# One FFN and attention kernel on one core: softmax in batches inside the attention turns, gathers ahead of the gate sums, row split one quarter later

## The reference

```python
def ffn(x):                       # x: (16384, 256)
    xn = x * rsqrt(mean(x * x) + eps) * norm_weight
    probs = softmax(xn @ router_w.T + router_b)          # 8 experts
    gates, idx = top_k(probs.T, cap)                     # cap = 2048 rows for each expert
    xe = xn[idx]
    hmid = gelu(einsum('ech,efh->ecf', xe, fc1_w) + fc1_b)      # 256 -> 1024
    ye = einsum('ecf,ehf->ech', hmid, fc2_w) + fc2_b            # 1024 -> 256
    out = zeros.at[idx].add(ye * gates)
    gate_sums = zeros.at[idx].add(gates)
    return out / maximum(gate_sums, 1e-9)

x = x + 0.5 * ffn(layernorm(x))
x = x + attention(layernorm(x))   # causal, per group of 512 rows, W_q, W_k, W_v, W_o
x = x + 0.5 * ffn(layernorm(x))
```

## Time and profile before

| | |
|---|---|
| median of 3 runs | 2108.49 us (2108.31 to 2108.55) |
| the profiled execution | 2110.22 us |
| its span, first to last instruction | 2108.4 us |
| mean granted TensorE clock | 0.954 |
| busy: TensorE, VectorE, ScalarE, GpSimd | 1920.1, 1472.9, 1423.7, 1239.9 us |

### The profile page before, as it was taken

The page is one execution under the profiler, slowest core; times in us unless marked ns, Lnnn a source line. Parts: engine busy times, 40 slices in busy tenths (PEclk is TensorE's granted clock), DMA queues, the critical chain, the costliest instruction groups (busy, mean ns, idle before and its releaser), DMA issues. The chain is left out here.

```text
span 2108.4 us, 41402 instructions
## 1 busy us (share of the span) xinstructions
PE 1920.1 (91%) x14844; PEld 1335.1 (63%) x14844; DVE 1472.9 (70%) x4305; ACT 1423.7 (68%) x2737; POOL 1239.9 (59%) x1353
## 2 busy tenths in 40 slices
PE   8628899999999999899999999238999999999997
PEld 6514556666666666577777777215666666666665
DVE  8788867677777765388888888787656555555542
ACT  8745556766767676578888887555676676666663
POOL 5213777677777776644444442024876767676665
PEclk9759999999999999999999999669999999999999
DMA  8932456464555454646555553215565655655443
GB/s 277 343 101 74 115 88 129 83 111 96 95 109 99 95 82 70 110 124 158 155 147 152 157 147 109 93 47 114 98 108 93 124 91 103 114 100 94 81 73 39
DMA packets 361742, 242.27 MB, mean 115 GB/s; under 512 B 228929, under 2 KB 348993, under 8 KB 361281
## 3 DMA queue, kind: packets, MB, share of 16 engines
q1 hardware_dynamic: 304192, 172.34, 31.0%
q0 software_dynamic: 57344, 67.29, 21.2%
HBM read 121.03 MB, written 84.93 MB: 98 GB/s over the span
## 5 line engine op out<-in xcount | busy, mean ns | idle before, releaser
L1251 DVE SCALAR_TENSOR_TENSOR hid_l<-hf,hid_h 128x512 f16<-128x512 f32 x512 | 351.2, 696 | 348.7 <-ACT hid_h L695 345.5
L1457 PE MATMUL ps<-w_h,hid_h 128*128 128x256 f16 x2048 | 558.8, 273 | 0.0
L1459 PE MATMUL ps<-w_h,hid_l 128*128 128x256 f16 x2048 | 558.7, 273 | 0.0
L1458 PE MATMUL ps<-w_l,hid_h 128*128 128x256 f16 x2048 | 558.7, 273 | 0.0
L799 ACT ACTIVATE hf<-ps,b 128x512 f32<-128x512 f32 x512 | 345.8, 675 | 83.5 <-PE ps L1459 76.4
L1457 PE MATMUL ps<-xt,w_h 128*128 128x512 f16 x1024 | 391.5, 382 | 8.3 <-ACT hf L799 8.3
L1458 PE MATMUL ps<-xt,w_h 128*128 128x512 f16 x1024 | 391.4, 382 | 0.0
L1459 PE MATMUL ps<-xt,w_l 128*128 128x512 f16 x1024 | 391.2, 382 | 0.0
L695 ACT ACTIVATE ys<-yb,weight 128x256 f32<-128x256 f32 x256 | 128.0, 506 | 344.3 <-DVE yb L1269 331.3
L695 ACT ACTIVATE hid_h<-hf 128x512 f16<-128x512 f32 x512 | 322.4, 630 | 16.2
L586 POOL DMA_INDIRECT weight<-gate_d,gate_at x256 | 257.6, 1006 | 82.1 <-issue 77.0
(11 more groups left out here) (295 smaller groups left out, 3879.9 us busy)
## 6 DMA issues: line engine op xcount, KB each, us to landing
w_st<-fc_t SPq DMA_DIRECT2D x32, 1024.0 KB, 5.6
xin<-x SPq DMA_DIRECT2D x32, 512.0 KB, 5.6
xa<-x_d SPq DMA_DIRECT2D x32, 512.0 KB, 4.5
out<-x SPq DMA_DIRECT2D x32, 512.0 KB, 5.2
z_d<-z SPq DMA_DIRECT2D x32, 512.0 KB, 6.0
xt<-xs SPq DMA_TRANSPOSE x256
weight<-gate_d,gate_at POOLq DMA_INDIRECT x256
b_st<-fc_b SPq DMA_DIRECT2D x16, 128.0 KB, 5.5
```

Of the source, the lines that this page charges most:

```text
L1251: dve.scalar_tensor_tensor(hid_l[:, n % 2, f, :], hf[:, f % HF, :], HS, hid_h[:, n % 2, f, :], ALU.mult, ALU.subtract).then_inc(s_hl, 1)
L1457: pe.matmul(dst, lh, rh, start=first, stop=False)
L1458: pe.matmul(dst, lh, rl, start=False, stop=False)
L1459: return pe.matmul(dst, ll, rh, start=False, stop=last)
```

## The change

Five things are changed.

1. Layer 1 gets four softmax batches (groups 0 to 16, 16 to 24, 24 to 28, 28 to 32). The first three run inside attention turns: shares_from in turns 22, 30 and 34, the exponential a turn later, shares two turns later. In route(1) seven of the eight transposes and the copy of 896 of 1024 columns run ahead of the fourth batch.
2. On GpSimd, both layers: the second half of the roots of chunk 0 stands between two halves of the gathers of chunk 1, the roots of chunk 1 right behind them, and the gathers of chunk 3 ahead of the gate sums; scatter(1) and scatter(2) go out in turns 3 and 4 ahead of the roots.
3. On VectorE: the statistics of chunk 1 ahead of count_slots(0, E0, 2), its shift ahead of the chunks; tile_of in two parts, one quarter ahead of the pick and three quarters behind the first quarter's work.
4. In layer 0, for m > 0: rows_hi, rows_shift and rows_lo of the next chunk in quarter 1 instead of quarter 0.
5. On TensorE: other_limits from quarter 3 of chunk 0 to quarter 0 of chunk 1.

```diff
@@ -83,7 +83,9 @@
     PER = P // NE
     RING = 4
     WIDE = 8
-    SOFT = (((0, 10), (10, 20), (20, 28), (28, 32)), ((0, 32),))
+    SOFT = (((0, 10), (10, 20), (20, 28), (28, 32)), ((0, 16), (16, 24), (24, 28), (28, 32)))
+    SOON = (22, 30, 34)
+    KEYED = NT // PER - 1
     assert KD == 2 and TG == 4 and NC == 4 and PER * NE == P and NT == P
 
     xf = x.rearrange("b s d -> (b s) d")
@@ -565,12 +567,12 @@
                 N0, E0 = layer * NC * NE, layer * NE
                 LAST = NC * NE
 
-                def gather(n):
+                def gather(n, t0=0, t1=TG):
                     E, c = divmod(n, NC)
                     pool.wait_ge(s_idx, n + 1)
                     wait(pool, s_xsl, TG * (n - 1))
                     pool.sem_inc(s_passed[0], 1)
-                    for t in range(TG):
+                    for t in range(t0, t1):
                         k = TG * c + t
                         landed = s_first[t] if n == N0 else s_xe[n % 2]
                         pool.indirect_dma_start(xe[:, n % 2, t, :], None, rows,
@@ -606,13 +608,14 @@
                     wait(pool, s_zst[u], 16 * (NG // 2) * layer)
                 gather(N0)
                 roots(N0, 0, TG // 2)
+                gather(N0 + 1, 0, TG // 2)
                 roots(N0, TG // 2, TG)
-                gather(N0 + 1)
+                gather(N0 + 1, TG // 2, TG)
+                roots(N0 + 1)
                 gather(N0 + 2)
-                roots(N0 + 1)
                 roots(N0 + 2)
+                gather(N0 + 3)
                 gate_sums(layer)
-                gather(N0 + 3)
                 gates(layer)
                 roots(N0 + 3)
                 pool.wait_ge(s_gate_d, 16 * (layer + 1))
@@ -626,6 +629,9 @@
                         gather(N0 + m + 2)
                     if m < LAST:
                         weights(N0 + m)
+                    early = scattered(m)[:1] if m in (3, 4) else []
+                    for n in early:
+                        scatter(N0 + n)
                     if m + 2 < LAST:
                         roots(N0 + m + 2)
                     if layer == 0 and m == LAST - 2:
@@ -641,7 +647,7 @@
                         first_factors(2)
                         scatter(m - 1, 2, TG)
                     else:
-                        for n in scattered(m):
+                        for n in scattered(m)[len(early):]:
                             scatter(N0 + n)
 
             def row_low(z):
@@ -732,11 +738,11 @@
                     exponents(0, (g - 16) // 10)
 
             def route(layer):
-                for b in range(2 - 2 * layer, len(SOFT[layer])):
+                for b in range(2 + layer, len(SOFT[layer])):
                     exponents(layer, b)
-                act.wait_ge(s_top, layer + 1)
+                act.wait_ge(s_top, 2 * layer + 1)
                 octets = flat(ps[1][:, :, :]).bitcast(U8).rearrange("p (n four) -> p n four", four=4)
-                act.wait_ge(s_pt, 2 * layer + 2)
+                act.wait_ge(s_pt, 3 * layer + 2)
                 for i in range(SEARCH):
                     part = sum(i >= o for o in OPENS) - 1
                     key = top[:, :].bitcast(I16) if part == 0 else keys[part - 1][:, :]
@@ -775,6 +781,9 @@
             def ffn(layer):
                 N0, E0 = layer * NC * NE, layer * NE
                 LAST = NC * NE
+
+                def soon(m):
+                    return 1 if layer == 0 and m > 0 else 0
 
                 def rows_hi(n):
                     if layer == 1 and n > N0:
@@ -840,7 +849,7 @@
                             gelu(n, 2 * t + 1)
                         for done, block in scaled(m, t):
                             y_out(N0 + done, block)
-                        if t == 0 and m + 1 < LAST:
+                        if t == soon(m) and m + 1 < LAST:
                             rows_hi(n + 1)
                         if ahead < E0 + NE:
                             if c == 1 and t % 2 == 1:
@@ -911,6 +920,8 @@
                     z_rows(z, 0)
                 if on(f) and c > EARLY:
                     hi_half(s_u, f, u_h, s_uh, 1)
+                if c - 1 in SOON:
+                    exponents(1, SOON.index(c - 1))
                 if on(a):
                     pth(a, 2)
                     pth(a, 3)
@@ -1042,18 +1053,20 @@
             def route(layer):
 
                 dve.tensor_copy(counts[:, :, P - 1], tile_at[:, :])
-                if layer == 1:
-                    shares_from(1, 0)
-                    shares(1, 0)
-
-                dve.wait_ge(s_pt, 2 * layer + 1)
-
-
                 p_top = flat(ps[1][:, :, :]).bitcast(BF16).rearrange("p (n two) -> p n two", two=2)[:, :, 1]
                 dve.memset(count[:, 2:3], 0.0)
                 dve.memset(signs[:, 0:1], 0.0)
-                dve.tensor_copy(top[:, :], p_top).then_inc(s_top, 1)
-                dve.wait_ge(s_top, layer + 1)
+                if layer == 0:
+                    dve.wait_ge(s_pt, 1)
+                    dve.tensor_copy(top[:, :], p_top).then_inc(s_top, 1)
+                else:
+                    dve.wait_ge(s_pt, 3)
+                    dve.tensor_copy(top[:, 0:KEYED * P], p_top[:, 0:KEYED * P]).then_inc(s_top, 1)
+                    shares_from(1, 3)
+                    shares(1, 3)
+                    dve.wait_ge(s_pt, 4)
+                    dve.tensor_copy(top[:, KEYED * P:KEYS], p_top[:, KEYED * P:KEYS]).then_inc(s_top, 1)
+                dve.wait_ge(s_top, 2 * layer + 1)
                 key, rounds = top, 0
                 for part in range(3):
                     ranked = top[:, :].bitcast(I16) if part == 0 else key[:, :]
@@ -1289,8 +1305,10 @@
                         choice_7(layer)
                     if (m, t) == (1, 3):
                         choice_8(layer)
+                        tiles(1, E0 + 1, 0, 1)
                         gate_scale(layer)
-                        tiles(1, E0 + 1)
+                    if (m, t) == (2, 0):
+                        tiles(1, E0 + 1, 1, NC)
                     if m >= 2 and t % 2 == 1:
                         count_slots(1, E0 + 1, 2 * (m - 2) + t // 2)
 
@@ -1315,34 +1333,38 @@
                 if layer == 1:
                     b2_rows(E0)
                 choice_1(layer)
+                rows_stats(N0 + 1)
                 count_slots(0, E0, 2)
                 if layer == 0:
                     router_halves()
                     attention_weights()
-                rows_stats(N0 + 1)
                 choice_2(layer)
                 for h in range(4):
                     w2_lo(E0, h)
+                rows_shift(N0 + 1)
                 for m in range(LAST + 1):
                     n = N0 + m
                     ahead, c = n // NC + 1, n % NC
                     more = ahead < E0 + NE
                     if more and c == 0 and m > 0:
-                        tiles(ahead - E0, ahead)
+                        tiles(ahead - E0, ahead, 0, 1)
                     for t in range(TG):
                         if m < LAST:
                             hidden_lo(n, 2 * t)
                             hidden_lo(n, 2 * t + 1)
                         if m >= 1:
                             y_bias(n - 1, t)
-                        if t == 0 and m + 1 < LAST:
-                            rows_shift(n + 1)
+                        if t == soon(m) and m + 1 < LAST:
+                            if m > 0:
+                                rows_shift(n + 1)
                             rows_lo(n + 1)
                         if m < NC:
                             first_turns(m, t)
                         if t == 3 and m + 2 < LAST:
                             rows_stats(n + 2)
                         if more:
+                            if m >= NC and (c, t) == (0, 0):
+                                tiles(ahead - E0, ahead, 1, NC)
                             if m >= NC and c < 2 and t % 2 == 1:
                                 count_slots(ahead - E0, ahead, 2 * c + t // 2)
                             if c == 2 and t < 2:
@@ -1441,6 +1463,10 @@
                     v_lo(f, 1)
                 if on(a):
                     residual(a, 3, v, ring)
+                if c in SOON:
+                    shares_from(1, SOON.index(c))
+                if c - 2 in SOON:
+                    shares(1, SOON.index(c - 2))
 
             for c in range(EARLY, NG + DEPTH):
                 att_turn(c)
@@ -1527,8 +1553,14 @@
                     lg(g - 2, g % 2)
 
             def route(layer):
-                pe.wait_ge(s_share, batch(layer, len(SOFT[layer]) - 1))
+                if layer == 1:
+                    pe.wait_ge(s_x2, TG * NG)
+                    pe.wait_ge(s_share, batch(1, 2))
                 for b in range(NT // PER):
+                    if b == layer * KEYED:
+                        if layer == 1:
+                            last.then_inc(s_pt, 1)
+                        pe.wait_ge(s_share, batch(layer, len(SOFT[layer]) - 1))
```

(3 more changed lines are left out.)

## The result

| | median | lowest to highest | runs |
|---|---|---|---|
| before | 2108.40 us | 2108.26 to 2108.55 | 4 |
| changed | 2135.20 us | 2133.07 to 2136.88 | 4 |

The changed kernel takes 1.0129 times as long (95% interval 1.0117 to 1.0141), 26.8 us more. The prediction said 2123.5 us, range 2105 to 2132: the sign was right, the size was missed by 11.7 us, and the time lies above the range. The profiled execution of the changed kernel took 2135.59 us, its span is 2133.9, and the span of the one before 2108.4: 25.5 us to explain.

A forecast was written before the change was run, and what follows sets the result against it. TensorE was taken as the bound, busy 543.5 of 546 us in the steady first FFN, so new waits are paid in full. Terms -5.8 + 1 + 2.6 + 12.8 - 2.5 + 4.5 + 2.6 = +15.2 gave 2123.5 us, range 2105 to 2132.

The forecast's parts named there:

- Route(1): Head of route(1) in layer 1: with three softmax batches done earlier, ScalarE's first count starts 5.8 us sooner (4.5 to 6.5).
- Attention: Attention turns: softmax work moved into six turns delays the next turn's maxima on VectorE; +1 us (0 to +3).
- Start of the first FFN: First chunks of the first FFN: later gate sums and w2 against stalls that go; net +2.6 us (-5 to +8).
- the w2 chain: Chunk 2, first FFN: later mask and gathers delay gate sums, w2 load, count_slots and the pick; +10 us.
- the 6.1 for scatter(2): First FFN near 293: scatter(2) a turn earlier removes a 4.4 us gelu wait and 1.7 of half pitch.
- The sentence with "-6.9" and "+2": Chunk 1, first FFN: the 3.9 gelu and 3.0 per_expert waits go (-6.9), a gather's length is lost twice (+2).
- Pick waits: First FFN, chunks 8 to 27: TensorE waits 1.28 us for count_slots in 10 chunks; +12.8 us (0 to +20).
- Tile waits: Steady part of the first FFN: five waits for tile_of go, since a quarter of it precedes the chunk; -2.5 us.
- Columns of the next chunk: Steady first FFN: transposes land late for TensorE in 15 chunks, 0.3 us each; +4.5 us (3 to 12).
- Second FFN: Start of the second FFN: gathers of chunk 3 ahead of the sums make w2 land later; +2.6 us (0 to +4).
- rival (c): Dearer: columns 0.8 late every chunk, picks 2.0 each, start +8, or clock falling behind picks; 2132 to 2143, chance 0.13.

The follow-up runs named there:

- the last experiment: Changed kernel with rows in quarter 0, gathers of chunk 3 behind the gate sums, and without the early scatters: 2096.3 us, against 2094.7 with them.
- The kernel with c = 2 and 3 alone: Changed kernel with the later rows in quarter 1 only in first-FFN chunks with c = 2 and 3, quarter 0 elsewhere: 2116.8 us.

## Why the prediction was wrong in size, step by step

- **Route(1): right.** Forecast -5.8, measured 13.7 less 7.8: -5.9. Attention: forecast +1; the last statistics come 29.1 us later (1360.91 against 1331.78) where chunk 32 of the FFN was 27.4 later: +1.7, within its range. The other -2.2 of the -6.4 arise between the first count and the end of chunk 1 of the second FFN, where the wait for per_expert (1.9 before) is gone; the prediction had no term for it.
- **Start of the first FFN: the w2 chain right, the scatter misread, 1.8 short.** The chain of the step, with its forecast and the measured times: sums done 216.2 and 213.9, w2 228.5 and 224.8, rows of chunk 3 done 235.4 and 233.2, count_slots 236.8 and 234.4, pick 236.9 and 234.6. All came two to four microseconds sooner, mostly since the gate sums took 5.1 us together, not 7.5 (the last one 0.46, not 2.05); the jump at chunk 2 is 9.4 us where 10 was forecast. What failed is the 6.1 for scatter(2). The prediction has it go out "a turn earlier"; the change has it in the same turn 4, only ahead of the roots, and it starts at 286.6, where it was 285.2 before. ScalarE still waits 5.0 us for it, and the pick behind it 3.0, where 1.5 was booked. With the rows back the last experiment prices both early scatters at 1.6. The sentence with "-6.9" and "+2" is in no sum: waits of 3.7 for the gelu and 3.0 for the columns of chunk 1 stand where 3.9 and 3.0 stood. The earlier trace rows also lacks a sixth wait of that window, 1.8 us for per_expert at L1562; no term used it.
- **Pick waits: right.** Forecast ten waits of 1.28; measured ten in the list, 11.5 us together, of at most 1.3 (13.1 counted from matmul start to matmul start, less the usual 0.11), with the chain at L+0.8, 1.2, 1.8, 5.1, 6.5 to within 0.1 of the text. The clock did not fall behind them: the granted clock of the stretch is 1.00. The Trainium skill, "TensorE: Matmul & The Clock Gate", section "Part 1: The HAM clock gate", lets an idle engine fall to half rate; the trace shows that behind the waits of 6.4 and 3.1 us in chunk 2 (granted clock 0.69 and 0.62 in the 4.3 and 4.2 us after them, that is mostly the lower of its two levels, 1.2 GHz), and not behind those of 1.3.
- **Tile waits: right.** Forecast -2.5, all five are gone (3.3, counted the same way).
- **Columns of the next chunk: this step failed.** It said "a matmul started 1.28 behind the end of such transfers", took 0.3 of 0.2 to 0.8 and 15 chunks: +4.5, bounds 3 to 12. Measured in the changed kernel it is 23.0 less 13.1 (the picks) plus 3.3 (the tile waits): **13.2**, 8.7 more than forecast, of the 10.3 that the span is above the sum. Of these 1.3 arise in turn 32, where the first columns of the transition come later as well (a wait of 3.65 us, 1.67 before), for which the prediction had no term; the rest is 0.8 per chunk, not 0.3. The kernel with c = 2 and 3 alone shows it without any pick wait: 11.3 us between chunks 6 and 32. The chain up to the issue was right: rows_hi at L+1.2, and in most chunks 5.1 us of issue that end at L+9.4. Wrong was the landing lag, taken from one quiet place of the transition and used as a constant. First use less end of issue is 1.87 in the mean, not 1.28. No wait of the trace before could tell it, since TensorE came 5.8 us behind the end of the issue; but the semaphore's updates show 2.7 in the mean there; with that as a constant the term would have been priced too high. So the lag is a range (1.2 to 4.1 us), and the forecast took its lower end. The code loads, by the single run with the code shifted, are some 3.6 of the 13.2; what makes up the rest of the lag stays open.
- **Second FFN: mis-sized.** Forecast +2.6, measured +4.5; w2 comes 4.3 later. The four gathers took 5.9 us (1464.51 to 1470.4), and the sums stand behind them in full.
- **Range.** Three terms came out too low together: 13.2 for 4.5 (bound 12), 4.5 for 2.6 (bound 4), 4.4 for 2.6 (bound 8). The first is the lag, the second the gathers (5.9 us, not 5.3) and the third the scatter, so no cause common to them was shown, and that all three fell on the same side may be chance. The forecasts of -5.8 and 12.8 came out to within 0.3. The rival (c), 2132 to 2143, which had the columns at 0.8 per chunk, is what happened, with a chance of 0.13; its other parts (picks of 2.0, the clock) did not.

## What to carry to other kernels

Before moving a producer by one turn, count its slack to the consumer with the landing time of its last transfer, as a range. A lag read in one quiet stretch is a lower bound; where no engine waits for the transfer, the updates of its semaphore in the same stage still give it. On an in-order engine the step lands behind everything of its new turn and ahead of everything queued after it, so both its own consumer and that of the next instruction have to be checked, and taking one wait away only shows the other. A wait that is removed at a start stage is worth the distance to the next releaser: here two of three (the load of w2, the scatter) gave back most of what they promised.

## What the runs showed of the hardware that was not expected

- Loads of instructions take part in the DMA traffic: one packet of 16 KB occupied a DMA engine for 1.1 to 1.5 us, and four transfers with such a packet among their last ones landed 2.8 to 3.4 us behind their issue, the others at most 1.8 (chunks 7 to 31 of the changed kernel). Moving the code by 135 instructions changed which transfers were hit and took 4.1 us out of the waits for columns (9.0 to 4.9), in a single run.
- The same four transposes landed 1.2 to 4.1 us behind the end of their issue within one stage of the kernel before (mean 2.7), though the issue itself took 5.1 to 5.4 us in most chunks.
- The same GpSimd sum of 128 x 128 took 2.05 us in the kernel before and 0.46 in the changed one (the row at 213.39), and nearly the same in the second FFN (2.05 and 0.45). The one of 128 x 512 took 1.80 and 1.26 in the first FFN, but 1.79 and 2.00 in the second. What VectorE ran beside them differs; whether that is the reason was not tested.
